# A four-layer network in one kernel: each sequence of the third layer beside the next sequence of the second

## The chip, the cores and the metric

One NeuronCore of a Trainium2 chip (trn2) runs the whole program in one launch. The metric is the device time of the kernel in microseconds (us), the median of the runs. The engines named are TensorE (PE, its weight loads PEld), VectorE (DVE), ScalarE (ACT), GpSimd (POOL) and SyncE (SP, which here only issues DMAs). Each takes its instructions in program order and meets the others at semaphores.

## What is computed

Four layers over `x` of 4 sequences x 512 tokens x 128 features, float32. Each layer normalises its input, computes a mixing branch `s` and a mixture of experts `g`, and adds their product:

```python
for layer in (0, 1, 2, 3):
    xn = layernorm(x)
    x = x + branch(xn) * silu(experts(xn))
```

Layer 0's branch is a selective scan, its experts are dense GELU experts. Layer 1 (the second, "causal"): 16 heads of 8 features, causal softmax attention, projection, residual and a layernorm; four live experts of width 704 with silu gating (22 pieces of 128 hidden units). Layer 2 (the third, "rope"): the numerator of its softmax takes rotated queries and keys, the denominator plain ones,

```python
att_num = exp(q_rope @ k_rope.T * scale)
att_den = exp(q @ k.T * scale).sum(-1, keepdims=True)
```

so all scores are formed twice; then projection, residual, layernorm, and eight experts of width 64. Layer 3: attention with ALiBi bias and capacity-routed top-1 experts over all tokens. A layer works on one sequence at a time and, for layers 0 to 2, needs nothing of the other sequences.

## The kernel before

Everything lies in SBUF: `x`, its normalised form `xn` and the transpose `xnt`. The order of the work is written out by hand: `flow` (L492) makes one list of items `(what, layer, sequence, n)`, and every engine walks that list and does its part of each item. So the list is the program order of all engines at once. The items of layers 1 and 2:

- `a` (layer 1 only): scores of two or four heads into one of two pairs of PSUM banks, whose row maxima DVE takes (`scores_a` L1023, `maxima` L1889). 20 for each sequence. `mx`: the maxima are transposed, split and go through DRAM into the key stacks (SP `maxima` L2220).
- `b`: scores again, to be exponentiated by ACT (`scores_b` L1073, `probabilities` L1470). 20 for a causal sequence. 64 for a rope sequence: for each of 4 head groups (quads) 8 "sums" units (two activations in place that give only row sums, L1480) and 8 rotated units (one activation of 1024 columns into SBUF, L1498).
- `pv`: probabilities times values, four heads side by side in the array, bank PV (`values` L1127); `bc`: transpose and division of a finished quad (L1154, L1919).
- `f`: one expert piece. In layer 1 two 512-column fp32 matmuls into banks MI and UP (L855, L856), a tanh on ACT (L1379), two DVE operations (L1675, L1679), and the down projection of the piece before it (L867). The next `f` may not begin before the second DVE operation has read bank MI. `q`, `v`, `gate` and the mixture's start use MI too.
- `q`: one projected operand, copied by ACT, split by DVE in three bf16 parts (L1867 to L1870), written to DRAM by SP and read back as "stacks" for the score matmuls (`parts_out` L2188, `stacks` L2201). Layer 2 has four, two of them with the rotation.
- `t`: the tail of a sequence in four steps: turn the heads, project (DVE: add, moments), branch norm and combine with the experts, normalise for the next layer and transpose (L1161, L1928, L1942, L1704, L1602, L836).

Layer 1 runs its four sequences one after the other, then layer 2 its four, then layer 3. `schedule` (L348) spreads `f` evenly over the `a` and `b` items, and `TAIL_AT`/`HEAD_AT` (L362) drop the tail of the sequence before and the head of the next between them. The banks are fixed: two pairs alternate over `a` and `b` units (`slot` L721), PV, UP, YB and MI serve the rest. Probabilities lie in two buffers of 4096 columns, `pt` (L587), and a causal quad's last key block in a small third one, `pty`. Layer 2's operands fill four stacks of 2048 columns for all 16 heads.

## Time and profile before

| | us |
|---|---|
| median of 3 runs | 2030.68 (2030.4 to 2031.54) |
| profiled execution | 2028.62 |
| its span | 2026.8 |
| layer 1: last transpose of layer 0 to layer 2's first scores | 493.8 to 1026.4 |
| layer 2: to layer 3's first scores | 1026.4 to 1542.0 |
| PE, DVE, ACT, POOL busy over the span | 1598.5, 1177.7, 1014.9, 209.7 |

The profile is one execution. Busy time of PE is modelled from pipelined matmuls. A view by windows gives the busy time of each engine in a stretch and the granted clock of PE as a share of 2.4 GHz; 0.50 in it is 1.2 GHz. In a timeline an entry is: start, duration, engine, line, operation, output and inputs, shape, count, and in brackets the idle time before it and what ended that. One fp32 matmul is recorded as two instructions.

### The profile page before, as it was taken

The page shows a single profiled execution, that of the slowest core. Times are in us where ns is not written, and L with a number is a line of the kernel's source. Part 1 is how long each engine was busy: PE and PEld are TensorE (multiplying, and loading weights), DVE is VectorE, ACT ScalarE, POOL GpSimd, SP SyncE. Part 2 cuts the span into 40 slices and gives each one's busy share as a digit, 9 for nine tenths or more (in the row PEclk, how much of TensorE's full clock was granted, in tenths as well). Part 3 has the DMA queues.
Part 4 walks back from the last instruction along what each step waited for, and adds up shares of the span by engine and source line. Part 5 has one row for each costly group of instructions (what it writes and reads, how often), then busy time and mean ns, then how long its engine had stood idle before and what let it go on. Part 6 is the DMA issues. An engine that isn't in the chain of part 4 may idle for free.

```text
span 2026.8 us, 24038 instructions
## 1 busy us (share of the span) xinstructions
PE 1598.5 (79%) x8656; PEld 786.6 (39%) x8656; DVE 1177.7 (58%) x2372; ACT 1014.9 (50%) x1658; POOL 209.7 (10%) x152
## 2 busy tenths in 40 slices
PE   5999999886897897888866777677675677786876
PEld 2655555553454444444422223232222322222342
DVE  4789899898646647557534233241225777573522
ACT  4786877772240321313357676666672122332675
POOL 1242423321000000000000000000000000001003
PEclk8999999997999999999978576566666677776999
DMA  5322322453020100100433012021020302021002
GB/s 172 99 79 76 85 73 79 120 136 99 2 63 1 49 17 2 55 8 2 123 110 103 24 32 79 16 82 43 0 67 12 84 28 72 14 72 44 1 2 68
DMA packets 91621, 116.30 MB, mean 57 GB/s; under 512 B 10096, under 2 KB 71536, under 8 KB 91120
## 3 DMA queue, kind: packets, MB, share of 16 engines
q1 hardware_dynamic: 89808, 110.05, 19.1%
q0 software_dynamic: 1696, 4.72, 0.8%
q8 instruction: 70, 1.15, 0.2%
q14 instruction: 47, 0.39, 0.1%
HBM read 83.27 MB, written 31.46 MB: 57 GB/s over the span
## 4 chain that ended last, share of the span: by engine, by line
PE 42%; DVE 19%; ACT 11%; issue 3%; DMA 1%; SPq 1%; POOL 1%; DVEq 0%; POOLq 0%; ACTq 0%
PE ps L1149 9%; PE ps L856 5%; PE ps L867 5%; DVE neg_max L1904 5%; PE ps L855 4%; ACT scratch L1498 4%; ACT ps L1480 3%; PE ps L1062 2%; PE ps L1013 2%; DVE gated L1675 2%; DVE hidden L1679 2%; ACT tanh L1379 1%; DVE mixture_sum L1701 1%; PE ps L1117 1%; ACT weights_even L1498 1%
## 5 line engine op out<-in xcount | busy, mean ns | idle before, releaser
L1498 ACT ACTIVATE scratch<-ps 128x1024 f32<-128x1024 f32 x272 | 274.4, 1021 | 237.3 <-PE ps L1119 61.4
L1904 DVE TENSOR_REDUCE neg_max<-ps 128x2 f32<-128x1024 f32 (+2 forms) x224 | 232.2, 1067 | 102.0 <-PE ps L1062 101.0
L1149 PE MATMUL ps<-scratch,values 128*32 128x512 f32 (+3 forms) x1280 | 186.8, 669 | 11.2 <-ACT scratch L1498 5.7
L1379 ACT ACTIVATE tanh<-ps 128x512 f32<-128x512 f32 x88 | 52.6, 597 | 282.0 <-PE ps L856 282.0
L1480 ACT ACTIVATE ps<-ps 128x512 f32<-128x512 f32 x256 | 150.8, 589 | 60.5 <-PE ps L1108 60.5
L1765 DVE TENSOR_TENSOR_SCAN scratch<-scratch 128x512 f32<-128x512 f32 x128 | 159.5, 1285 | 3.6 <-ACT scratch L1451 3.5
L1675 DVE SCALAR_TENSOR_TENSOR gated<-tanh,ps 128x512 f32<-128x512 f32 x88 | 60.4, 686 | 154.2 <-ACT tanh L1379 154.1
L1917 DVE COPY head_out<-ps 128x512 f32<-128x512 f32 x48 | 33.0, 688 | 191.7 <-PE ps L1149 191.4
L878 PE MATMUL ps<-xnt,weights_even 128*128 128x512 f32 x256 | 127.2, 619 | 7.4 <-ACT gated L1362 6.6
L2085 POOL TENSOR_SCALAR variance_eps<-mean_var 128x4 f32<-128x4 f32 x20 | 5.3, 265 | 1079.0 <-DVE mean_var L1596 1079.0
L855 PE MATMUL ps<-xnt,weights_odd 128*128 128x512 f32 x176 | 105.3, 682 | 12.7 <-DVE hidden L1679 8.7
L867 PEld LDWEIGHTS ps<-weights_odd,hidden 128*128 128x128 f32 x640 | 88.4, 201 | 46.2 <-issue 40.4
L1498 ACT ACTIVATE weights_even<-ps 128x1024 f32<-128x1024 f32 x64 | 65.1, 1024 | 79.9 <-PE ps L1123 79.5
L1117 PE MATMUL ps<-scratch 48*128 48x512 bf16 x256 | 69.5, 516 | 41.9 <-ACT scratch L1498 35.0
L1108 PE MATMUL ps<-scratch 48*128 48x512 bf16 x256 | 73.3, 519 | 37.1 <-ACT ps L1480 36.6
L856 PE MATMUL ps<-xnt,weights_odd 128*128 128x512 f32 x176 | 97.3, 637 | 0.0
L1701 DVE SCALAR_TENSOR_TENSOR mixture_sum<-ps,combine,mixture_sum 128x128 f32<-128x128 f32 x176 | 49.5, 344 | 82.1 <-PE ps L867 82.1
L1062 PE MATMUL ps<-scratch 52*128 52x256 bf16 (+7 forms) x704 | 94.1, 336 | 0.0
L867 PE MATMUL ps<-weights_odd,hidden 128*128 128x128 f32 x640 | 88.6, 284 | 5.0 <-DVE hidden L1679 5.0
L2124 POOL TENSOR_TENSOR weights_odd<-weights_odd,scratch 128x512 f32<-128x512 f32 x32 | 74.7, 2333 | 168.5 <-DVE scratch L1772 168.1
L1048 PE MATMUL ps<-consts,scratch 128*128 128x128 bf16 x256 | 42.5, 257 | 56.9 <-DVE neg_max L1904 56.6
L2124 POOL TENSOR_TENSOR scratch<-scratch 128x512 f32<-128x512 f32 x32 | 67.8, 2120 | 131.8 <-DVE scratch L1772 131.7
(316 smaller groups left out, 2945.2 us busy)
## 6 DMA issues: line engine op xcount, KB each, us to landing
scratch<-state_rows SPq DMA_DIRECT2D x64, 512.0 KB, 4.7
scratch<-parts_scratch SPq DMA_DIRECT2D x288, 96.0 KB, 2.3
parts_scratch<-weights_even SPq DMA_DIRECT2D x168, 128.0 KB, 2.4
weights_odd<-in_l SPq DMA_DIRECT2D x8, 519.5 KB, 6.4
weights_even<-in_l SPq DMA_DIRECT2D x1, 4096.0 KB, 15.7
weights_odd<-in_l SPq DMA_DIRECT2D x1, 4096.0 KB, 14.8
parts_scratch<-gated SPq DMA_DIRECT2D x15, 128.0 KB, 2.4
slots_scratch<-head_out SPq DMA_DIRECT2D x5, 256.0 KB, 5.0
```

The lines of the kernel that those rows point to most:

```text
L855: pe.matmul(ps[:, MI, :], W(l, "w3")[:, P * f:P * (f + 1)], tokens(b), start=True, stop=True)
L856: pe.matmul(ps[:, UP, :], w1, tokens(b), start=True, stop=True).then_inc(q[l, "up_ready"], 1)
L867: mm = pe.matmul(ps[:, YB, P * j:P * (j + 1)], buf[lo:lo + n, P * j:P * (j + 1)], W(l, "w2")[lo:lo + n, P * src:P * (src + 1)], start=(one ...
L878: pe.matmul(ps[:, up_bank(0, n), :], W(0, "w1")[:, P * f:P * (f + 1)], tokens(n // NF[0]), start=True, stop=True).then_inc(q[0, "up_ready" ...
L1062: mm = pe.matmul(place(col + c0, c1 - c0), lhs, stack_of(l, b, 1 + turn)[p0:p0 + KA[l], s, c0:c1], start=False, stop=True, skip_group_chec ...
L1149: mm = pe.matmul(ps[32 * i:32 * i + 32, PV, q0:q0 + n], lhs, buf[:, slot, col:col + n], start=first_, stop=True, skip_group_check=True)
L1480: ins = act.activation(bank, bank, ACT.Exp, accum_out=dens[:, j, h:h + 1])
L1498: act.activation(dst, src, ACT.Exp).then_inc(q[l, "exp_done"], 1)
L1675: own.link(stt(act_g[:, :], act_t[:, :], 1.0, ps[:, UP, :], ALU.add, ALU.mult))
L1765: dve.tensor_tensor_scan(hs[:, g, :], da[n % RING][:, g, :], ub[:, g, :], 0.0, ALU.mult, ALU.add)\
L1904: ins = dve.tensor_reduce(dst, ps[:, base:base + 2, col:col + n], AX.X, ALU.max, negate=True)
L2124: pool.tensor_tensor(y1[b % 2], y1[b % 2], hc[n % 3][:, 1, :], ALU.add)\
```

## The change

`flow` no longer runs layer 1 and then layer 2. After layer 0 it emits `causal_alone` (layer 1, sequence 0), then for b = 1, 2, 3 `causal_beside_rope(b)`, a block with sequence b of layer 1 and sequence c = b - 1 of layer 2, and then `rope_alone` (layer 2, sequence 3). The last quad of a rope sequence and its tail spill into the next block; so does the tail of the causal sequence, on which the rope sequence of the same block depends. `weave` merges lists evenly. What goes with it:

- Score units of both layers alternate over the same two PSUM pairs in list order. Both layers share MI, UP, YB and PV; waits for these banks are now kept in one variable each.
- The two probability buffers become a ring of four buffers of 2048 columns (`ring`, `grain`), filled stage by stage by either layer; a stage is now one key block (one or two for causal).
- Rope sums come before the rotated units in every quad. Layer 2's stacks shrink to two quads (`stack2`); SP loads each quad by an item `ld`, after the quad two before it has been scored. Parts of layer 2 go through two buffers for four operands, in the order q, rotated q, k, rotated k.
- Layer 2's expert pieces become `u2` (up) and `d2` (down and mix, one per expert). Their buffers, layer 2's `heads` and layer 1's combine weights move to free columns of the even weights.
- POOL serves the reciprocal deviations in list order instead of in loops; semaphores are shared by the parity of the layer.

The arithmetic per layer, the matmuls, activations and DVE operations stay the same in number and shape, apart from layer 1's `pv`, which has the same four key blocks in three stages.

```diff
+GRAINS = 4
+OPERAND = {1: (0, 1), 2: (0, 2, 1, 3), 3: (0, 1)}
...
-            for n, hp in enumerate(pairs):
+            for hp in pairs:
                 units_a.append([(h, 3, 512 * k, 512) for k, h in enumerate(hp)])
                 units_a.append([r for k, h in enumerate(hp)
                                 for r in ((h, 2, 512 * k, 384), (h, 0, 512 * k + 384, 128))])
-                units_b.append((len(stages), 2 * n, [(h, 0, 512 * k, 512) for k, h in enumerate(hp)]))
-                units_b.append((len(stages), 2 * n + 1, [r for k, h in enumerate(hp)
-                                                         for r in ((h, 1, 512 * k, 384), (h, 3, 512 * k + 384, 128))]))
-            stages.append((g, "x", len(units_b), 3))
             units_a.append([(h, 1, 256 * n, 256) for n, h in enumerate(by_parity(hs))])
+            for n, hp in enumerate(pairs):
+                units_b.append((len(stages), n, [(h, 0, 512 * k, 512) for k, h in enumerate(hp)]))
+            stages.append((g, [(0, 0, 0, 512)], len(units_b)))
+            for n, hp in enumerate(pairs):
+                units_b.append((len(stages), n, [r for k, h in enumerate(hp)
+                                                 for r in ((h, 1, 512 * k, 384), (h, 3, 512 * k + 384, 128))]))
+            stages.append((g, [(1, 128, 0, 384), (3, 384, 384, 128)], len(units_b)))
             units_b.append((len(stages), 0, [(h, 2, 256 * n, 256) for n, h in enumerate(by_parity(hs))]))
-            stages.append((g, "y", len(units_b), 1))
+            stages.append((g, [(2, 256, 0, 256)], len(units_b)))
+        elif kind == "rope":
+            sums = [[(h, j, 512 * k, 512) for k, h in enumerate(hp)] for j in range(TB) for hp in pairs]
+            units_b += [(None, 0, unit) for unit in sums]
+            for j in range(TB):
+                for n in range(2):
+                    units_b.append((len(stages), n, sums[2 * j + n]))
+                stages.append((g, [(j, 0, 0, 512)], len(units_b)))
...
-def schedule(l):
-    f = [("f", n) for n in range(NF.get(l, 0))]
-    a = [("a", u) for u in range(len(score_units(KIND[l])[0]))]
-    b = b_items(KIND[l])
-    if l == 1:
-        return spread(a, f[:7]) + [("mx", 0)] + f[7:9] + spread(b, f[9:]) + [("fl", 0)]
-    if l == 2:
-        return b[:12] + [("mb", 0)] + b[12:14] + f[:1] + spread(b[14:-16], f[1:]) + [("fl", 0)] + b[-16:]
-    raise ValueError(l)
-TAIL_AT = {1: (1, 4, 32, 47), 2: (1, 3, 6, 10)}
-HEAD_AT = {1: (("q", 0, 36), ("q", 1, 40), ("v", 0, 44), ("gate", 0, 49), ("cw", 0, 52)),
-           2: (("q", 0, 30), ("q", 1, 36), ("q", 2, 42), ("q", 3, 48), ("v", 0, 54), ("gate", 0, 58), ("cw", 0, 62))}
...
+HEAD = {1: (("q", 0), ("q", 1), ("gate", 0), ("cw", 0), ("v", 0)),
+        2: (("q", 0), ("q", 1), ("q", 2), ("q", 3), ("v", 0), ("gate", 0), ("cw", 0))}
...
+def weave(*lists):
+    at_ = [((2 * n + 1) / (2 * len(items)), k, n) for k, items in enumerate(lists) for n in range(len(items))]
+    return [lists[k][n] for _, k, n in sorted(at_)]
+def causal_group(b, g):
+    u = [("b", 1, b, 5 * g + n) for n in range(5)]
+    pv = [("pv", 1, b, 3 * g + n) for n in range(3)]
+    return u[0:4] + pv[0:1] + u[4:5] + pv[1:3], ("bc", 1, b, g)
+def rope_sums(b, g):
+    return [("b", 2, b, 16 * g + n) for n in range(8)]
+def rope_group(b, g):
+    u = [("b", 2, b, 16 * g + 8 + n) for n in range(8)]
+    pv = [("pv", 2, b, 4 * g + n) for n in range(4)]
+    return u[0:4] + pv[0:1] + u[4:6] + pv[1:2] + u[6:8] + pv[2:4], ("bc", 2, b, g)
+def later(items, item, n=2):
+    return items[:n] + [item] + items[n:]
+def causal_alone():
+    a = [("a", 1, 0, n) for n in range(20)]
+    f = [("f", 1, 0, n) for n in range(NF[1])]
+    out = weave(a, f[0:7]) + [("mx", 1, 0, 0)] + f[7:9]
+    main, bc = [], None
+    for g in range(QUADS):
+        group, next_bc = causal_group(0, g)
+        main += later(group, bc) if bc else group
+        bc = next_bc
+    head = head_items(1, 1)
+    return out + weave(main, f[9:], head[:4]) + [("fl", 1, 0, 0), bc] + [("ld", 1, 1, g) for g in range(3)]
+def causal_beside_rope(b):
+    c, p = b - 1, b - 2
+    a = [("a", 1, b, n) for n in range(20)]
+    f = [("f", 1, b, n) for n in range(NF[1])]
+    tail1 = [("t", 1, b - 1, k) for k in range(4)]
+    tail2 = [("t", 2, p, k) for k in range(4)] if p >= 0 else []
+    d = [("d2", 2, p, e) for e in range(4, E2)] if p >= 0 else [None] * 4
+    head1, head2 = head_items(1, b + 1) if b + 1 < NB else [], head_items(2, c)
+    group, bc = rope_group(p, 3) if p >= 0 else ([], None)
+    sums = rope_sums(p, 3) if p >= 0 else []
+    out = [("ld", 1, b, 3), d[0]] + weave(a[0:3], f[0:1], tail1[0:2], sums[0:3])
+    out += [d[1]] + weave(a[3:6], f[1:3], sums[3:8])
+    out += weave(a[6:12], f[3:6], group, tail1[2:4], [("v", 1, b, 0)])
+    out += [f[6], bc, d[2], a[12]] + tail2[0:1] + [head2[0], a[13], d[3]] + tail2[1:2]
+    out += weave(f[7:10], head2[1:5]) + [("ld", 2, c, 0), ("ld", 2, c, 1)] + tail2[2:3]
+    out += weave(a[14:18], f[10:12], head2[5:7], tail2[3:4])
+    group, bc = rope_group(c, 0)
+    out += weave(rope_sums(c, 0), a[18:20] + [("mx", 1, b, 0)], [("mb0", 2, c, 0), ("mb1", 2, c, 0)])
+    d = [("d2", 2, c, e) for e in range(4)]
+    out += [("u2", 2, c, 0), group[0], ("u2", 2, c, 1)] + group[1:3] + [d[0]] + group[3:5] + [d[1]]
+    out += weave(group[5:], f[12:16])
+    group, last = causal_group(b, 0)
+    out += later(weave(group, f[16:17], rope_sums(c, 1)), bc)
+    group, bc = rope_group(c, 1)
+    out += [("ld", 2, c, 2)] + later(weave(group, f[17:18]), last)
+    group, last = causal_group(b, 1)
+    sums = rope_sums(c, 2)
+    out += [d[2]] + later(weave(group, sums[0:4]), bc) + [d[3]]
+    group, bc = causal_group(b, 2)
+    out += later(weave(group, sums[4:8], f[18:20], head1[0:1]), last) + [("ld", 2, c, 3)]
+    group, last = rope_group(c, 2)
+    out += later(weave(group, f[20:22], head1[1:2]), bc)
+    group, bc = causal_group(b, 3)
+    out += later(weave(group, [("u2", 2, c, 2), ("u2", 2, c, 3)]), last) + [("fl", 1, b, 0)] + head1[2:4] + [bc]
+    if b + 1 < NB:
+        out += [("ld", 1, b + 1, g) for g in range(3)]
+    return [item for item in out if item]
+def rope_alone():
+    c, p = NB - 1, NB - 2
+    tail1, tail2 = [[("t", l, b, k) for k in range(4)] for l, b in ((1, c), (2, p))]
+    d = [("d2", 2, p, e) for e in range(4, E2)]
+    head = head_items(2, c)
+    group, bc = rope_group(p, 3)
+    out = weave(rope_sums(p, 3), tail1[0:2], d[0:2]) + weave(group, tail1[2:4])
+    out += [head[0], bc, d[2], head[1], head[2], d[3], head[3]] + tail2[0:1] + [head[4]] + tail2[1:2] + head[5:7]
+    out += [("ld", 2, c, 0), ("ld", 2, c, 1)] + tail2[2:4]
+    next_ = [("set", 3, 0, 0), ("q", 3, 0, 0), ("q", 3, 0, 1), ("v", 3, 0, 0)]
+    d = [("d2", 2, c, e) for e in range(E2)]
+    u = [("u2", 2, c, n) for n in range(4)]
+    beside = [[("mb0", 2, c, 0), ("mb1", 2, c, 0)], u[0:2] + d[0:2], [("ld", 2, c, 2)] + d[2:4],
+              u[2:4] + d[4:6], [("ld", 2, c, 3)] + d[6:8] + next_[0:1], next_[1:2], next_[2:3], next_[3:4]]
+    bc = None
+    for g in range(QUADS):
+        group, next_bc = rope_group(c, g)
+        sums = rope_sums(c, g)
+        out += weave(later(sums, bc) if bc else sums, beside[2 * g]) + weave(group, beside[2 * g + 1])
+        bc = next_bc
+    return out + [bc], [("t", 2, c, k) for k in range(4)]
+def flow():
+    middle, tail = rope_alone()
+    out = first_layer(head_items(1, 0)) + causal_alone()
+    for b in range(1, NB):
+        out += causal_beside_rope(b)
+    return out + middle + last_layer(tail)
...
+        stack2 = [scratch[:, 4096 + 1024 * n:4096 + 1024 * (n + 1)].bitcast(BF16).rearrange("p (s t) -> p s t", t=T)
+                  for n in range(4)]
+        ring = [scratch[:, 8192 + 2048 * n:8192 + 2048 * (n + 1)].rearrange("p (i c) -> p i c", i=4) for n in range(GRAINS)]
...
+        slots, grains, free_when = {}, {}, []
+        for what, l, b, n in steps:
+            if what in ("a", "b") and l in (1, 2):
+                slots[what, l, b, n] = len(slots) % 2
+                stage = units[l][1][n][0] if what == "b" else None
+                if stage is not None and (l, b, stage) not in grains:
+                    grains[l, b, stage] = len(free_when)
+                    free_when.append((l, NS[l] * b + stage + 1))
...
+                def grain_values(l, b, s):
+                    st = units[l][2]
+                    g, regions, end = st[s]
+                    first_ = s == 0 or st[s - 1][0] != g
+                    pe.wait_ge(q[l, "exp_done"], start[l, "exp_done"] + b * NUB[l] + end + 2)
+                    if first_:
+                        pe.wait_ge(*pv_read)
+                        if s == 0:
+                            pe.wait_ge(q[l, "values_ready"], start[l, "values_ready"] + b + 1)
+                    for c, q0, col, n in regions:
                         for i in range(4):
                             h = 4 * g + i
-                            lhs = vx[b % 2][:, c, VW * h:VW * h + 32]
-                            slot = by_parity(range(4)).index(i) if what == "y" else i
-                            mm = pe.matmul(ps[32 * i:32 * i + 32, PV, q0:q0 + n], lhs, buf[:, slot, col:col + n],
+                            place_ = by_parity(range(4)).index(i) if l == 1 and c == 2 else i
+                            mm = pe.matmul(ps[32 * i:32 * i + 32, PV, q0:q0 + n], vx[l - 1][:, c, VW * h:VW * h + 32],
+                                           grain(l, b, s)[:, place_, col:col + n],
                                            start=first_, stop=True, skip_group_check=True)
-                    if part == parts - 1:
-                        mm.then_inc(q[l, "pv_done"], 1)
+                    mm.then_inc(q[l, "pv_done"], 1)
...
+                        place_ = grains[l, b, s]
+                        if n == 0 and place_ >= GRAINS:
+                            from_, count = free_when[place_ - GRAINS]
+                            act.wait_ge(q[from_, "pv_done"], start[from_, "pv_done"] + count + (2 if from_ == 1 else 0))
...
+            def rope_stack(b, g):
+                l, n = 2, QUADS * b + g
+                if n >= 2:
+                    sp.wait_ge(q[l, "b_ready"], 16 * (n - 1))
+                for k in range(4):
+                    sp.wait_ge(q[l, f"parts{k}_out"], 16 * NG * (b + 1))
+                    quad_in(l, b, k, g, stack2[k], 2 * (g % 2), q[l, f"rotated{g}_in" if k >= 2 else f"stack{g}_in"])
...
+            for what, l, b, n in steps:
+                if what == "q" and l < 3:
+                    part_out(l, b, n)
+                    if l == 1 and b == 0 and n == 1:
+                        for g in range(QUADS):
+                            causal_stack(0, g)
+                        sp.wait_ge(xn_ready[0], NB)
+                        load_weights(2)
+                elif what == "ld":
+                    if l == 1:
+                        causal_stack(b, n)
+                    else:
+                        rope_stack(b, n)
+                elif what == "mx" and l == 1:
+                    maxima(1, b)
+                elif what == "t" and l == 1 and n == 3 and b == NB - 1:
+                    sp.wait_ge(xn_ready[1], NB)
+                    load_weights(3)
+                    rows(3)
```

## Rows read from the trace of the kernel before

**Rows 1.** The page: busy tenths of PE, and its clock, in 40 slices.

```profile
PE   5999999886897897888866777677675677786876
...
PEclk8999999997999999999978576566666677776999
```

**Rows 2.** Windows: stretch, length, busy us per engine, PE clock, DMA share, GB/s.

```profile
493.80:1026.40 532.60, 452.20 (x2866) 250.66 (x2865) 321.98 (x657) 144.64 (x192) 7.60 (x12) 0.96 0.12 34
493.80:620.00 126.20, 110.45 (x700) 60.07 (x699) 70.46 (x134) 35.00 (x46) 0.00 (x0) 0.95 0.13 39
1026.40:1542.00 515.60, 364.69 (x1576) 135.20 (x1575) 154.99 (x476) 345.42 (x717) 10.13 (x16) 0.66 0.19 55
626.00:670.00 44.00, 34.55 (x204) 19.42 (x200) 35.30 (x56) 4.35 (x8) 1.27 (x2) 0.92 0.01 1
714.00:758.00 44.00, 39.13 (x278) 22.07 (x274) 17.95 (x35) 14.09 (x18) 0.00 (x0) 1.00 0.07 19
1138.00:1146.00 8.00, 4.98 (x20) 0.74 (x18) 0.00 (x0) 6.52 (x15) 0.00 (x0) 0.50 0.10 32
1170.90:1300.50 129.60, 91.91 (x396) 34.29 (x397) 41.14 (x127) 86.61 (x180) 2.53 (x4) 0.66 0.18 49
```

**Rows 3.** Timeline, PE, layer 1: first and third of three pieces, then scores.

```profile
662.01 1.12 PE L855 MATMUL ps<-xnt,weights_odd 128*128 128x512 f32 x2
...
670.40 1.10 PE L855 MATMUL ps<-xnt,weights_odd 128*128 128x512 f32 x2 [1.33 <-DVE hidden L1679]
...
673.08 0.28 PE L1098 MATMUL ps<-consts 128*128 128x128 bf16 x2
```

**Rows 4.** Timeline, PE, layer 2: sums alone, a dense place, pv at half clock.

```profile
1032.74 0.61 PE L1108 MATMUL ps<-scratch 48*128 48x512 bf16 x2 [0.81 <-ACT ps L1480]
...
1033.95 0.61 PE L1108 MATMUL ps<-scratch 48*128 48x512 bf16 x2 [0.60 <-ACT ps L1480]
...
1063.22 0.39 PE L1108 MATMUL ps<-scratch 48*128 48x512 bf16 x2
...
1114.77 1.93 PE L1149 MATMUL ps<-scratch,values 128*32 128x512 f32 x8
```

**Rows 5.** DVE, layer 1: groups by form; first and last step of a split.

```profile
L1675 DVE SCALAR_TENSOR_TENSOR gated<-tanh,ps 128x512 f32<-128x512 f32 x88 | 60.4, 686 | 154.2 <-ACT tanh L1379 154.1
...
L1904 DVE TENSOR_REDUCE neg_max<-ps 128x2 f32<-128x1024 f32 x32 | 38.9, 1217 | 0.9 <-PE ps L1062 0.9
L1904 DVE TENSOR_REDUCE neg_max<-ps 128x2 f32<-128x768 f32 x32 | 30.4, 950 | 0.1
L1896 DVE TENSOR_REDUCE neg_max<-ps 128x4 f32<-128x1024 f32 x16 | 19.4, 1210 | 0.2 <-PE ps L1062 0.2
L1904 DVE TENSOR_REDUCE neg_max<-ps 128x2 f32<-128x256 f32 x32 | 13.3, 415 | 0.0
...
684.14 0.43 DVE L1867 CAST weights_even<-queries_keys 128x512 bf16<-128x512 f32 x1 [1.97 <-ACT queries_keys L1467]
...
685.79 0.69 DVE L1870 TENSOR_TENSOR weights_even<-queries_keys,weights_even 128x512 bf16<-128x512 f32 x1
```

**Rows 6.** ACT: three exponentials in a row (layer 1); table loads (layer 2).

```profile
673.72 2.85 ACT L1498 ACTIVATE scratch<-ps 128x1024 f32<-128x1024 f32 x3 [0.73 <-PE ps L1114]
...
L1383 ACT ACT_TABLE_LOAD x16 | 20.5, 1283 | 0.3
```

**Rows 7.** Timeline, DVE: first, a middle and last step of layer 1's last tail.

```profile
1031.44 0.69 DVE L1934 TENSOR_TENSOR branch<-ps,weights_odd 128x512 f32<-128x512 f32 x1 [3.31 <-PE ps L1170]
...
1035.97 1.11 DVE L1945 TENSOR_SCALAR branch<-branch,mean_var,rstd 128x128 f32<-128x128 f32 x4 [1.58 <-POOL rstd L2086]
...
1044.99 0.43 DVE L1609 TENSOR_SCALAR branch<-xn 128x512 f32<-128x512 f32 x1
```

**Rows 8.** SP queue: layer 2, four operands out, then back as stacks.

```profile
961.58 31.11 SPq L2199 DMA_DIRECT2D parts_scratch<-weights_even  x24
...
992.80 20.08 SPq L2216 DMA_DIRECT2D scratch<-parts_scratch  x32
```

490 lines of the change are left out of this document (243 added, 247 removed).

## Prediction, made before the change was run

> **What bounds the kernel now.** I read the page's slices first, then windows by layer, then timelines inside them. The slices show three regimes [rows 1]: PE 0.8 to 0.9 busy at full clock up to slice 20, then a stretch of clock digits 5 to 8. Windows put layers on them [rows 2]. Layer 1 takes 532.6 us, with PE 452.2 busy at clock 0.96, DVE 322.0, ACT 144.6. Layer 2 takes 515.6 us, with PE 364.7 busy at clock 0.66, DVE 155.0, ACT 345.4. So layer 1 lives by PE, with ACT nearly free; layer 2 is a mix of ACT and a PE that runs half of its time at 1.2 GHz, with DVE free. The two have different scarce engines, and that is what the change bears on.
>
> PE work is best counted at full clock: busy times clock, 452.2 x 0.96 = 434 us for layer 1 and 364.7 x 0.66 = 241 us for layer 2, so 108.5 and 60.3 us for each sequence. A sequence pair now takes (532.6 + 515.6) / 4 = 262 us for 169 us of such work, a yield of 0.64. Alone, layer 1 yields 434 / 532.6 = 0.81, layer 2 only 0.47.
>
> Inside layer 1 there is a second limit. The first and the third of three expert pieces in a row begin at 662.01 and 670.40 [rows 3]: 4.2 us for one, while PE needs 2.7 us for one (670.40 to 673.08). The rest is the way through tanh and two DVE operations back to bank MI. 22 pieces at 4.2 us are 92 us of a sequence. In the first half of a sequence, where `a` units use DVE, DVE is 35.3 busy of 44 us and PE 34.6 (at 0.92); in the second half PE 39.1 of 44 at 1.00 [rows 2]. In layer 2 sums units come every 1.2 us, set by ACT, with PE 0.61 us at half clock [rows 4].
>
> **What the change removes.** Nothing in work: the same matmuls, activations, reductions, and 8 table loads of 1.28 us for each rope sequence [rows 6] (a GELU and the exponential after it, each piece still by itself). What it can remove is idle time and half-clock time of PE. If three pairs ran together at PE's full-clock work alone they would take 3 x 169 us; nothing lets them go below.
>
> **One block, stretch by stretch.** Prices: causal score unit 0.65 us of PE (an estimate, near the 0.6 that one bias-and-scores unit takes from 673.08 on at full clock), rope unit 0.3 (0.39 with its pipeline [rows 4]), rope `pv` 1.0 (1.93 at half clock [rows 4]), a piece 2.7, `q` or `v` 1.0. On ACT 1.2 for a sums unit, 0.95 for an exponential [rows 6]. On DVE 1.28 for an `a` unit ((38.9 + 30.4 + 19.4 + 13.3) / 80), 1.4 for a piece (twice 0.69), 2.3 for a split (684.14 to 686.48) and 2.1 more (three operations of 0.69) with rotation [rows 5], 14.0 for the tail of a causal sequence (1031.44 to 1045.42 [rows 7]), of which 3.2 wait for POOL (two waits like the 1.58 there).
> (1) Opening to `f` 5: DVE has 12 `a` (15.4), 6 pieces (8.4), the causal tail (10.8 without the waits), values and two expert mixes (some 4): 38.6 us. At the 0.80 busy that DVE reaches in layer 1's first half [rows 2] this is 48; ACT's share (16 rope units, 17 us) hides in it. 47.
> (2) `f` 6 to 9, four `q`, `v`, start of the rope tail: everything but PV work goes through bank MI. Four pieces at 4.2, four `q` and a `v` at about 2, and two rotated splits of 4.4 us that lie on DVE ahead of a piece's operations. In order I get 37 us for 20 us of PE work. 37.
> (3) End of the rope tail, 4 `a`, 2 pieces, gate: DVE 6 + 5.1 + 2.8 + 5 + 1.6 = 20.5. 21.
> (4) Sums of the new sequence: 8 x 1.2 on ACT. 11.
> (5) Two GELUs with four table loads between exponentials (10 on ACT), then four pieces at 4.2. 27.
> (6) The rest, 4 causal quads, 2 rope quads, 16 sums units, 6 pieces: PE 68, ACT 63, DVE 20. At a PE yield of 0.85 (0.89 in layer 1's second half, where only one stream of exponentials had to keep step) 80.
> Sum 223 us at full clock.
>
> **The clock.** Stretches 2 to 4 hold some 35 us of PE work in 69 us. Layer 1's first half held 0.92 with PE 0.79 busy; layer 2 sat at 0.50 in 1138 to 1146 with PE 4.98 of 8 busy, so half that in full-clock work [rows 2]. A stretch at a load of 0.5 lies between the two rows, nearer to the second. Bounds: nothing, or all 35 us doubled (+35). Since ACT and DVE set most of these steps, I add 3 us in full blocks: **226**. The yield is then 169 / 226 = 0.75, between layer 1's 0.81 and today's 0.64. The Trainium skill has the rule behind this (TensorE: Matmul & The Clock Gate, Part 1: The HAM clock gate): the slow clock is the resting state and activity lifts it, so thinning PE's work costs twice. By it alone the block goes as rival D.
>
> **The first block** has no older rope sequence: no spilled quad (8.9 us of PE), no four expert downs, no rope tail on DVE (10.8). 226 less some 20: 206.
>
> **The ends.** `causal_alone` is today's first sequence, 493.8 to 620 [rows 2]: 126. `rope_alone` is worse off than today's last sequence. Today its operands are ready long before. Now a spilled quad (17 us of ACT, an estimated 20 with the causal tail's 14 us and its matmuls beside it), then four `q` with 13.4 us of splits that each wait for their copy (20), then the rope tail, `v` and gate on DVE (17) stand ahead of its first sums, with ACT idle: 57. The 4 MB of layer 3's weights is issued in just that place; bounds nothing to 10 us, and I take nothing, as the splits' DMAs have those 17 us of cover. The main part: today's 129.6 [rows 2] less the head's 5 matmuls of 2 us at half clock, the tail's stall and matmuls (some 14): 104. Sum 161.
>
> **Stacks and SP.** A block issues 36 DMAs of parts, 48 of stacks and 3 of maxima. Issues take 0.4 us when nothing holds them and 0.63 in the run of 32 [rows 8]: at most 55 us in 226, no bound. From the last split to the first sums unit lie 10 issues and two landings, some 10 us, under stretch 3's 21. An item `ld` waits on scores done long before. Behind SP's wait for the maxima stands only the next `ld`, a stretch later. Nothing; if the cover fails, up to 10 a block. The ring of four half-size buffers holds as much as two old ones, and the price of its cross-layer wait is bounded by 0 and by one `pv` (1 us) in 12 stages a block; a gain is excluded as it never frees earlier than its own stage. I take 0. POOL's services in list order are two of 1.6 us as now.
>
> **Sum.** 126 + 206 + 2 x 226 + 161 = 945 against 1048.2 (layers 1 and 2 [rows 2]): 103 less. Layer 3 begins the same way. 2028.6 - 103 = 1925.6 for an execution like the profiled one; the median lies 2.1 above it: 1927.7, so **1928**.
>
> **Rivals.**
> B, the streams decouple better: with four consumers of PE's work the yield rises to 0.85, near layer 1's second half. Full block 199, first 150 / 0.85 = 176, ends 126 + 155: 855, saving 193: 1838. For it: stretches 1 and 6 want different engines. Against: the 4.2 us of a piece and the one bank MI. The Trainium skill goes further (Perfetto Trace Analysis, Identifying the Most-Contended Engine): not matmul busy but weight-load busy shows PE's headroom. By it PE has more than half left in both layers (250.7 of 532.6, 135.2 of 515.6 [rows 2]). That would make a block some 150, bound by DVE and ACT (119 and 122 us for a pair), and the time near 1700; I give this nothing, since three pieces' matmuls in [rows 3] fill their 2.7 us each.
> C, coupling: one order over two pairs means that a DVE unit held up by a tail keeps ACT's next unit out. Yield 0.68: blocks 248, first 222, ends 126 + 170: 1014, saving 34: 1997. This also holds late stacks (three times 10) as its smaller form.
> D, slower: the clock falls through the block. Blocks then keep layer 2's clock 0.66 with PE 0.93 busy, a yield of 0.62: 273, first 250, ends 126 + 175: 1097, costing 49: 2080. It decides from a yield of (3 x 169 - 19) / (1048 - 287) = 0.64. For it: stretches 2 to 4 at half load, and layer 3, also mixed, with clock digits 6 to 9 [rows 1]. Against: layer 1's first half kept 0.92 [rows 2].
> E, the change doesn't do what it says: if every rope item waited on the causal tail of its own block, the layers would run in turn as before, 2030. The tail ends in the first third of a block, so this is thin.
>
> **How the numbers follow.** The chances: forecast 0.60 (blocks of 213 to 240, 1885 to 1970), B 0.14, C 0.14, D 0.09, E 0.03. Range: down to 1855 takes half of B, up to 2000 most of C; left out are some 0.07 below and 0.13 above. 0.2% (4 us) is about what a measurement of this kernel can tell from no change. Faster 0.60 + 0.14 + 0.14 = 0.88, same 0.03, slower 0.09.
>
> **What would show it.** In the changed kernel's windows, from layer 0's last transpose to layer 3's first scores: 945 us; blocks of 206, 226, 226; clock 0.9 over them, lower in each block's second and third stretch; DVE 0.8 busy in each block's first 100 us and under 0.3 after; ACT idle for some 35 us at the start of `rope_alone`. Wrong if the blocks' clock is under 0.75, if PE waits for stack DMAs by more than 10 us a block, or if the blocks' second part is as slow as the first.

## The result, and the profile of the changed kernel

The changed kernel takes **2075.66 us** (median of 4 runs, 2071.7 to 2081.96) against 2030.54 us (2028.87 to 2031.54) for the kernel before on the same chip: a ratio of 1.0232, 95% interval 1.0209 to 1.0256. It is 2.3% slower where the forecast had it 5% faster. The profiled execution spans 2069.9 us, the one before 2026.8: 43.1 us more. Of these 4.5 lie ahead of layer 1's first scores, 35.1 in layers 1 and 2 (1083.3 us against 1048.2 [rows 2]) and 3.5 in layer 3.

The page's slices of TensorE and of its clock, to be laid beside [rows 1]:

```profile
PE   5999899896796678876788776887486677675876
...
PEclk8999999997998878977689786897557568777899
```

Before, layer 1 had a clock digit of 9 throughout, and the low digits stood in layer 2 and in layer 3 behind it. Now digits of 5 to 8 begin with slice 13, where block 1 begins, and run, with a few of 9 among them, through both layers. They have only moved: over both layers the granted clock is 0.81 in either kernel.

Windows of the changed kernel (columns as in [rows 2]): both layers, `causal_alone`, the three blocks, `rope_alone`, then block 2 in the prediction's six stretches:

```profile
498.30:1581.60 1083.30, 829.21 (x4443) 402.76 (x4441) 478.56 (x1137) 492.33 (x908) 18.76 (x28) 0.81 0.14 42
498.30:629.00 130.70, 112.63 (x704) 61.77 (x702) 71.83 (x138) 34.48 (x45) 0.00 (x0) 0.93 0.10 31
629.00:862.00 233.00, 179.29 (x1012) 88.28 (x1011) 107.35 (x249) 105.43 (x189) 2.53 (x4) 0.86 0.15 42
862.00:1135.00 273.00, 211.36 (x1117) 103.70 (x1117) 122.33 (x298) 124.00 (x228) 5.58 (x8) 0.81 0.13 36
1135.00:1408.00 273.00, 209.67 (x1110) 101.99 (x1109) 116.47 (x269) 125.66 (x235) 5.59 (x8) 0.81 0.08 24
1408.00:1581.60 173.60, 116.26 (x505) 47.01 (x506) 60.58 (x188) 102.77 (x212) 5.06 (x8) 0.66 0.29 89
862.00:930.00 68.00, 52.66 (x234) 25.91 (x233) 35.80 (x74) 22.27 (x45) 2.53 (x4) 0.75 0.00 1
930.00:968.00 38.00, 25.12 (x101) 14.54 (x101) 26.21 (x56) 5.89 (x10) 1.79 (x2) 0.82 0.25 67
968.00:997.00 29.00, 17.73 (x87) 10.46 (x86) 19.36 (x64) 3.31 (x8) 1.26 (x2) 0.71 0.27 77
997.00:1012.00 15.00, 10.62 (x40) 4.18 (x38) 4.94 (x7) 10.68 (x30) 0.00 (x0) 0.54 0.01 2
1012.00:1044.00 32.00, 27.45 (x126) 13.81 (x126) 8.67 (x19) 16.40 (x19) 0.00 (x0) 0.79 0.09 26
1044.00:1135.00 91.00, 77.78 (x537) 34.79 (x536) 27.35 (x80) 65.44 (x118) 0.00 (x0) 0.92 0.16 44
```

Block 2 takes 273 us where I had 226. It splits into three terms that will be used throughout: work at full clock 211.36 x 0.81 = 171 us, half-clock time 211.36 - 171 = 40 us, idle 273 - 211.36 = 62 us. A pair of sequences before, from [rows 2], has 204 busy, of which 169 of work and 35 of half-clock time, and 58 idle. So the change removed neither of the two losses. Against the kernel before, most of what it adds over both layers is idle time: 254 us for 231, and busy time 829 for 817.

```profile
493.80:1542.00 1048.20, 816.89 (x4438) 385.86 (x4437) 476.97 (x1133) 490.06 (x909) 17.73 (x28) 0.81 0.15 45
```

Where the half-clock time now falls, by groups of layer 1's up products (first the two of the changed kernel, then the one of the kernel before that answers to L975; columns: group, busy us, mean ns, idle before):

```profile
L975 PE MATMUL ps<-xnt,weights_odd 128*128 128x512 f32 x176 | 125.0, 799 | 17.6 <-DVE hidden L1832 8.5 <-ACT weights_even L1620 6.7 <-DVE values L2043 1.4
L976 PE MATMUL ps<-xnt,weights_odd 128*128 128x512 f32 x176 | 112.4, 726 | 0.0
```

```profile
L855 PE MATMUL ps<-xnt,weights_odd 128*128 128x512 f32 x176 | 105.3, 682 | 12.7 <-DVE hidden L1679 8.7 <-DVE values L1886 1.2 <-ACT queries_keys L1467 0.9
```

The same 88 up products (176 recorded instructions) cost 20 us more. And the timeline of TensorE in block 3 and in `rope_alone` (start, us, instruction, idle before it and what ended it):

```profile
1182.22 1.01 PE L1149 MATMUL ps<-weights_odd,xnt 128*128 128x128 f32 x3 [4.27 <-DVE hidden L1832]
...
1191.75 1.08 PE L963 MATMUL ps<-consts,branch 128*128 128x128 f32 x4 [2.90 <-DVE branch L1762]
...
1223.98 2.08 PE L1143 MATMUL ps<-xnt,weights_even 128*128 128x512 f32 x2 [5.57 <-DVE hidden L1832]
...
1226.80 2.07 PE L975 MATMUL ps<-xnt,weights_odd 128*128 128x512 f32 x2 [0.75 <-ACT weights_even L1620]
...
1251.28 1.03 PE L969 MATMUL ps<-weights_even,xnt 128*128 128x8 f32 x4 [4.05 <-DVE hidden L1832]
...
1471.63 1.08 PE L963 MATMUL ps<-consts,branch 128*128 128x128 f32 x4 [12.96 <-DVE branch L1762]
```

`v` (L1149), `q` (L1143), gate (L969) and the turned normalised input (L963) all need bank MI or the tail's result, and each waits 3 to 13 us for VectorE. Behind such a wait one up product (x2, as it is recorded as two instructions) takes 2.07 us (1.2 GHz); in a dense place it takes 1.12, as in [rows 3]. Added over block 2, waits ended by `hidden` are 18.4 us, by `neg_max` (layer 1's maxima, which free a pair of score banks) 10.1 and by `branch` 6.9; in two sequences of the kernel before (755 to 888 and 1170.9 to 1300.5) they are 5.2, 8.5 and 8.1. What is new is the wait for `hidden`. (The expectations below give 18.9 and 10.8 for the block's `hidden` and `branch`; the trace has 18.4 and 6.9.)

### The profile page after: what moved, and what is told of

It reads as the page before. It is cut to its first block, busy times and chain, and to the rows that moved or that the text cites. A ratio compares the mean times of both kernels' runs of the same rounds, so it can differ in the third digit from the quotient of the medians.

```text
span 2069.9 us, 24003 instructions
## 1 busy us (share of the span) xinstructions
PE 1603.0 (77%) x8656; PEld 804.5 (39%) x8656; DVE 1177.8 (57%) x2370; ACT 1017.4 (49%) x1658; POOL 210.0 (10%) x152
## 4 chain that ended last, share of the span: by engine, by line
PE 38%; DVE 20%; ACT 13%; issue 4%; DMA 1%; SPq 1%; POOL 0%; DVEq 0%; ACTq 0%; POOLq 0%
DVE neg_max L2061 6%; PE ps L975 5%; PE ps L1292 5%; PE ps L995 4%; PE ps L976 4%; ACT scratch L1650 4%; ACT ps L1633 3%; PE ps L1273 2%; PE ps L1192 2%; PE ps L1143 2%; DVE gated L1828 1%; PE ps L1238 1%; PE ps L1242 1%; ACT weights_even L1650 1%; DVE hidden L1832 1%
## 5 line engine op out<-in xcount | busy, mean ns | idle before, releaser
L975 PE MATMUL ps<-xnt,weights_odd 128*128 128x512 f32 x176 | 125.0, 799 | 17.6 <-DVE hidden L1832 8.5
L1292 PE MATMUL ps<-scratch,values 128*32 128x512 f32 (+3 forms) x1024 | 131.1, 604 | 4.3 <-ACT scratch L1650 3.8
L995 PEld LDWEIGHTS ps<-weights_odd,hidden 128*128 128x128 f32 x640 | 98.3, 220 | 52.1 <-issue 51.0
L976 PE MATMUL ps<-xnt,weights_odd 128*128 128x512 f32 x176 | 112.4, 726 | 0.0
L995 PE MATMUL ps<-weights_odd,hidden 128*128 128x128 f32 x640 | 96.2, 300 | 0.7 <-DVE hidden L1832 0.7
L1242 PE MATMUL ps<-scratch 48*128 48x512 bf16 x256 | 61.6, 460 | 38.2 <-ACT scratch L1650 21.7
L1238 PE MATMUL ps<-scratch 48*128 48x512 bf16 x256 | 62.6, 473 | 31.1 <-ACT ps L1633 20.2
L1854 DVE SCALAR_TENSOR_TENSOR mixture_sum<-ps,combine,mixture_sum 128x128 f32<-128x128 f32 x128 | 35.9, 343 | 88.8 <-PE ps L995 88.8
```

Of the source, the lines that this page charges most:

```text
L975: pe.matmul(ps[:, MI, :], W(l, "w3")[:, P * f:P * (f + 1)], tokens(b), start=True, stop=True)
L976: pe.matmul(ps[:, UP, :], W(l, "w1")[:, P * f:P * (f + 1)], tokens(b), start=True, stop=True)\
L995: mm = pe.matmul(ps[:, YB, P * j:P * (j + 1)], buf[lo:lo + n, P * j:P * (j + 1)], W(l, "w2")[lo:lo + n, P * src:P * (src + 1)], start=(one ...
L1238: mm = pe.matmul(place(col, n), stack2[0][p0:p0 + rows_, s % 4, P * c:P * (c + 1)], stack2[1][p0:p0 + rows_, s % 4, :], start=True, stop=True)
L1292: mm = pe.matmul(ps[32 * i:32 * i + 32, PV, q0:q0 + n], vx[l - 1][:, c, VW * h:VW * h + 32], grain(l, b, s)[:, place_, col:col + n], start ...
```

## The experiments

Three theories were open. **Clock**: half-clock time is what the block loses, and would come back if TensorE were kept busy. **Parts**: the ring, the stacks and the quad-wise sums cost, not the order. **Chains**: in one order, VectorE's tail of one layer stands ahead of what the other layer's bank MI needs; TensorE waits, and the clock falls behind the wait.

**The parts without the order.** All of the change, but `flow` gives four sequences of layer 1 (the block's list without layer 2's items) and then four of layer 2 (`rope_in_turn`: four quads as in `rope_alone`, with tail and head of the neighbours beside them).

```diff
+def causal_in_turn(b):
+
+    out = [item for item in causal_beside_rope(b) if item[1] == 1]
...
     out = first_layer(head_items(1, 0)) + causal_alone()
     for b in range(1, NB):
-        out += causal_beside_rope(b)
-    return out + middle + last_layer(tail)
+        out += causal_in_turn(b)
+    for c in range(NB):
+        out += rope_in_turn(c)
+    return out + last_layer([("t", 2, NB - 1, k) for k in range(4)])
```

> The changed kernel with its new parts (ring of four half buffers, stacks of layer 2 apart, quad-wise sums) but the two layers in turn: four sequences of layer 1, then four of layer 2. Clock theory (the changed order costs because thin, gapped TensorE work now also strikes layer 1's fp32 products): layer 1 keeps its granted clock of about 0.95 and some 131 us a sequence, layer 2 some 129 to 140 us at a clock of 0.66, in all 2020 to 2060 us, and layer 1's up products (with the down products behind them) at full clock as before. Parts theory (the ring, the stacks and the sums cost, not the order): 2075 us or more, with the loss inside layer 2's sequences, at 140 us or more each. Order-and-tails theory (VectorE's tails now stand in the path of both layers): like the clock theory here, 2020 to 2060; what tells these two apart are the filled kernels.

Measured 2067.1 us (ratio 1.0184, 1.0158 to 1.0211). One sequence of each layer:

```profile
780.00:933.00 153.00, 118.13 (x719) 65.46 (x718) 80.87 (x170) 35.67 (x48) 2.53 (x4) 0.91 0.08 22
...
1236.80:1355.50 118.70, 85.71 (x396) 31.33 (x396) 40.77 (x127) 86.87 (x180) 2.53 (x4) 0.67 0.19 54
```

All three expectations missed, in the total, which lies 7 us above the one range and 8 below the other, and inside. Layer 2 is 11 us a sequence *faster* than before at the same clock (118.7 against 129.6 [rows 2]), so the parts are a gain there. Layer 1 is 20 us slower, with 35 idle, of which 18.8 for `hidden`: the list that is left when layer 2's items are taken out of a block is a bad one for layer 1. A pair costs 271.7 us here, nearly the block's 273, though nothing is interleaved.

**The same, with layer 1 in its old order.** Heads and tails back at their old places among layer 1's items, `vx` and `faccs` taken by sequence again.

```diff
+    main = weave(a, f[0:7]) + [("mx", 1, b, 0)] + f[7:9] + weave(stream, f[9:]) + [("fl", 1, b, 0)]
...
+        extras += [(-1, ("ld", 1, b, 3))] + [(at_, ("t", 1, b - 1, k)) for k, at_ in enumerate((1, 4, 32, 46))]
...
+        extras += [(at_, item) for at_, item in zip((36, 40, 44, 48, 51), head_items(1, b + 1))]
```

> The layers in turn with the new parts, as in the first of these kernels (layer 2 there took 118.5 us a sequence against 129.6 to 133.4 before), but layer 1's items in the order of the kernel before: heads and tails each at their old places among the scores, two value buffers and two mixture sums taken by sequence. Theory that the interleaving costs and the parts gain: layer 1 takes 131 to 135 us a sequence again instead of 153, layer 2 117 to 121, together 1000 to 1012 us against 1048 before and 1083 with the interleaving, in all 1980 to 2000 us. Parts theory (the ring, stacks and sums cost something in layer 1, and 153 us was theirs): 145 us or more a sequence of layer 1, 2030 us or more in all.

Measured **2009.28 us**, ratio 0.990 (0.9872 to 0.9929): faster than both kernels. The sequences are as expected; the total is 9 us above what was expected, the two layers taking 1017 us. Second sequence of layer 1, second of layer 2:

```profile
624.60:757.00 132.40, 110.18 (x723) 62.12 (x721) 80.61 (x170) 35.61 (x48) 2.53 (x4) 0.97 0.09 25
...
1179.30:1298.90 119.60, 87.44 (x397) 30.96 (x397) 40.87 (x127) 86.99 (x180) 2.53 (x4) 0.67 0.19 53
```

The pair costs 252 us. Beside that, not beside 262, stands the block's 273: the interleaved order costs 21 us a block. The parts theory has fallen. Since the pair of the first kernel in turn costs 271.7 us with the block's order of layer 1 and no item of layer 2 in it, the 21 us need not come from having both layers in one list; they can as well come from where the block puts layer 1's heads, tails and hidden tiles among its scores. These runs do not tell the two apart.

**Which part gains in layer 2.** Its ring cut from four half buffers to two.

```diff
-GRAINS = 4
+GRAINS = 2
```

> The kernel with the layers in turn and tuned (2009 us), but with a ring of two half buffers instead of four. Theory that the ring is what makes layer 2 faster (119.6 us a sequence against 129.6 to 133.4): layer 2 goes back to 128 us or more and the whole to 2045 us or more, layer 1 loses too. Theory that the order of the sums (a whole quad of them ahead of its rotated units) makes it: layer 2 stays within 119 to 123 us, layer 1 loses at most 3 us a sequence, 2009 to 2035 us in all.

2013.07 us (ratio 0.988, 0.9843 to 0.9917), and a sequence of layer 2 takes the same:

```profile
1174.20:1293.70 119.50, 86.89 (x397) 31.02 (x397) 40.86 (x127) 87.00 (x180) 2.53 (x4) 0.67 0.19 53
```

So the ring is not the gain. What is left is the order of the sums (a quad of them ahead of its rotated units, not one by one) with its stacks, and the expert pieces of layer 2, cut into `u2` and `d2` and put at other places: waits for `mixture_sum` are 6.3 us in the old sequence and 0.5 in the new one. None of these was run apart.

**Filling TensorE's queue.** Matmuls by a tile of zeros, added into a bank that TensorE holds anyway, ahead of the long waits; then many more; then the same in layer 2 of the kernel before.

```diff
+            def warm(bank, n):
+                for _ in range(n):
+                    pe.matmul(ps[0:64, bank, :], small[:, 16:48].bitcast(BF16), c16[:, 0:T], start=False, stop=True,
+                              skip_group_check=True)
...
```

> The changed kernel plus matmuls by a weight tile of zeros, 512 columns of bf16 each, added into a PSUM bank that TensorE holds anyway: 6 ahead of each q, 8 ahead of each v, gate and turned xn of layers 1 and 2 (56 to 64 in each of the three blocks, 1 to 2 us ahead of each of those waits). They do no work that is needed. Clock theory: some of the 42 us a block that the half clock costs come back and little is paid, since they run in idle time: blocks at a granted clock of 0.86 to 0.92 instead of 0.81 and 255 to 268 us instead of 273, in all 2020 to 2062 us. Waiting theory (idle time on VectorE's chain is the loss, the clock only follows it): clock up a little, blocks 273 to 285 us, 2075 to 2110 us.

> As the kernel before it, plus one such matmul behind each unit of scores and two behind each down product while a bank is held: about 170 in a block, 37 us of TensorE time at full clock and 73 at half. Clock theory: the granted clock goes to 0.95 or more in the blocks; with 169 + 37 us of work at full clock and 62 us of waits of which half is now filled a block takes 235 to 255 us, in all 1965 to 2025 us. Waiting theory: the added work comes on top, 285 to 310 us a block, 2110 to 2190 us.

> The kernel before with three such matmuls behind each unit of layer 2's scores while the accumulating bank is held, 29 places in a sequence, 87 matmuls, 19 us at full clock and 38 at half. Clock theory: layer 2 gets a granted clock of 0.8 to 0.95 instead of 0.66, but ScalarE (345 us of 516 busy) and its own chain hold its pace: 118 to 129 us a sequence, in all 1985 to 2030 us. Rival (the added time is paid in full, clock or no clock): 135 to 145 us a sequence, 2055 to 2095 us.

Measured 2063.35 us (ratio 1.0164, 1.0145 to 1.0184), 2100.86 (1.0339, 1.0303 to 1.0375) and 2038.94 (1.0049, 1.0028 to 1.0069). Block 2 of the second of them, then its fillers alone:

```profile
885.00:1162.00 277.00, 244.11 (x1291) 114.21 (x1290) 122.69 (x298) 124.29 (x228) 5.59 (x8) 0.88 0.12 35
```

```profile
885.00:1162.00 277.00, 55.73 (x172) 17.29 (x172) 0.88 0.12 35
```

The clock went from 0.81 to 0.88, and the busy time of the needed matmuls from 211 to 244.1 - 55.7 = 188 us: 23 us came back, and 29 of idle time were covered. The fillers' 56 us ate both, since half of them did not land in a wait. The light form is 12 us below the changed kernel by the medians, at the near edge of what the clock theory gave it. In layer 2 of the kernel before the clock rose from 0.66 to 0.78, and the needed busy time fell from 365 to 309 us:

```profile
1026.00:1548.00 522.00, 409.33 (x1914) 155.00 (x1914) 153.91 (x472) 346.52 (x715) 10.13 (x16) 0.78 0.19 55
```

```profile
1026.00:1548.00 522.00, 100.76 (x348) 29.36 (x348) 0.78 0.19 55
```

Yet it takes 522 us instead of 515.6. The clock theory, as a cause that can be treated by itself, missed by 1, by 76 and by 9 us, and the theory of plain waiting missed too, by 9 to 16 us at the other side: a fast clock bought with more work gives little or nothing. The light form, too, brought waits down, those for `branch` in block 2 from 6.9 to 1.5 us.

**The order of the block.** The same 206 items. First: layer 1's scores 4 to 17 stand one by one between the items that use MI, and its `v` and parts of its tail come earlier. Then one step more: the hidden tile and `v` go ahead of layer 2's tail, and layer 2's sums behind it, in the place of layer 1's scores. `t2` and `t3` are parts 2 and 3 of layer 2's tail.

```diff
...
-    out += weave(f[7:10], head2[1:5]) + [("ld", 2, c, 0), ("ld", 2, c, 1)] + tail2[2:3]
-    out += weave(a[14:18], f[10:12], head2[5:7], tail2[3:4])
+    out += [a[10], f[7], a[11], head2[1], a[12], f[8], a[13], head2[2], a[14], head2[3]] + t2
+    out += [a[15], f[9], a[16], head2[4], ("ld", 2, c, 0), ("ld", 2, c, 1), a[17], f[10], head2[5]] + t3 + [f[11], head2[6]]
```

```diff
-    out += [a[10], f[7], a[11], head2[1], a[12], f[8], a[13], head2[2], a[14], head2[3]] + t2
-    out += [a[15], f[9], a[16], head2[4], ("ld", 2, c, 0), ("ld", 2, c, 1), a[17], f[10], head2[5]] + t3 + [f[11], head2[6]]
+    out += [a[10], f[7], a[11], head2[1], a[12], f[8], a[13], head2[2], a[14], head2[3], ("ld", 2, c, 0), ("ld", 2, c, 1)]
+    s = rope_sums(c, 0)
+    out += [f[9], a[15], a[16], head2[4], a[17]] + t2 + s[0:3] + [f[10], s[3], head2[5], s[4], f[11], head2[6]] + t3
     group, bc = rope_group(c, 0)
-    out += weave(rope_sums(c, 0), a[18:20] + [("mx", 1, b, 0)], [("mb0", 2, c, 0), ("mb1", 2, c, 0)])
+    out += [a[18], s[5], ("mb0", 2, c, 0), a[19], s[6], ("mx", 1, b, 0), ("mb1", 2, c, 0), s[7]]
```

> The changed kernel with the same 206 items in a block, in another order in its first 130 us: layer 1's scores 4 to 17 are kept back and put one by one between the items that all use the bank MI (hidden tiles, q, v, gate, turned xn), which in the changed kernel stand right behind each other. Coupling theory (the block loses by chains through one bank: 18.9 us of waits for hidden and 10.8 for branch in block 2, against 5.2 and 8.1 in the two sequences apart): 12 to 18 us of these go, blocks of 254 to 262 us, in all 2020 to 2048 us. Clock theory: the same work spread evenly over the stretch, so a granted clock of 0.85 or more and up to 10 us more back, 2000 to 2030 us. Rival (TensorE's idle time belongs to the sum of the two layers' chains and only moves): 268 to 276 us a block, 2065 to 2085 us.

> The reordered block (259.5 us, 2041 us in all) with one more step: in its trace TensorE waits 11.6 us ahead of v of layer 2, for a hidden tile that VectorE does only after the whole tail of layer 2's sequence before. So that tile and v go ahead of this tail, the stacks are loaded earlier, and layer 2's sums, which only ScalarE has to release, stand behind the tail instead of layer 1's scores, which need VectorE. Coupling theory: 8 to 12 us of this wait go, blocks 2 and 3 at 247 to 253 us and 2015 to 2030 us in all. Rival (the wait moves to the next item that needs VectorE): 257 to 262 us, 2036 to 2046 us.

Measured 2041.4 us (ratio 1.0049, 1.0023 to 1.0074) and 2022.16 us (0.9921, 0.9897 to 0.9945): both times are as the chain theory had them, and the second is below the kernel before. In the first the mechanism was another one. Of the 12 to 18 us that were to go from the waits for `hidden` and `branch`, next to nothing went: they are 18.9 and 5.9 us a block, for 18.4 and 6.9. What fell are the waits for `neg_max`, from 10.1 to 1.3 us: TensorE hardly meets score banks any more whose maxima VectorE has not taken. So the chain through MI was not what this reordering shortened, and its time was right by luck. The second reordering did shorten it: `hidden` fell to 10.4, while `branch` went up to 7.1 and 4.8 us of waiting for layer 2's stacks were new. Block 2 of each:

```profile
855.00:1114.50 259.50, 204.64 (x1119) 99.45 (x1117) 122.15 (x299) 123.85 (x229) 5.07 (x8) 0.82 0.13 37
```

```profile
850.00:1099.90 249.90, 198.71 (x1117) 96.71 (x1116) 121.68 (x297) 123.52 (x229) 5.06 (x8) 0.85 0.14 39
```

How such a chain looks, in the first of the two. TensorE at `v`, and VectorE in the time ahead of it:

```profile
954.03 2.08 PE L1154 MATMUL ps<-weights_even,xnt 128*128 128x128 f32 x8 [11.57 <-DVE hidden L1837]
```

```profile
945.08 1.11 DVE L2107 TENSOR_SCALAR branch<-branch,mean_var,rstd 128x128 f32<-128x128 f32 x4
...
949.13 0.69 DVE L1877 SCALAR_TENSOR_TENSOR x<-branch,x 128x512 f32<-128x512 f32 x1
...
951.47 1.19 DVE L2066 TENSOR_REDUCE neg_max<-ps 128x2 f32<-128x1024 f32 x1
952.58 0.68 DVE L1833 SCALAR_TENSOR_TENSOR gated<-tanh,ps 128x512 f32<-128x512 f32 x1
953.29 0.69 DVE L1837 SCALAR_TENSOR_TENSOR hidden<-gated,ps 128x512 f32<-128x512 f32 x1
```

The two operations that free MI (952.58, 953.29) take 1.4 us, and stand in VectorE's queue behind two splits and the third part of layer 2's tail, which keep it busy without a gap from 937.1 on. In the second kernel the same wait is 3.07 us.

**Fillers again, on the first reordering** (49 in a block).

> The kernel of the reordered block with 47 to 51 matmuls of zero weights added in a block: 3 ahead of each q, v and gate, 4 ahead of each turned xn, one behind each down product while its bank is held. Clock theory: 10 us more of half-clock time go for some 11 us of added matmuls, most of it in idle time: 5 to 10 us a block less than without, 1990 to 2030 us in all. Rival (what is added is paid): the same time as without the fillers or up to 12 us a block more.

2048.75 us (ratio 1.0086, 1.0056 to 1.0115), by the medians 7 us more than without (the two intervals overlap), so the clock theory missed and the rival held. Block 2: clock 0.86 instead of 0.82, and 0.9 us longer.

```profile
862.40:1122.80 260.40, 212.24 (x1168) 101.27 (x1167) 122.17 (x297) 123.83 (x228) 5.06 (x8) 0.86 0.13 37
```

**The same step at the end.** `rope_alone` reordered likewise: sums between gate, tail and turned input, stacks loaded right behind the last `q`.

```diff
-    out += [head[0], bc, d[2], head[1], head[2], d[3], head[3]] + tail2[0:1] + [head[4]] + tail2[1:2] + head[5:7]
-    out += [("ld", 2, c, 0), ("ld", 2, c, 1)] + tail2[2:4]
+    out += [head[0], bc, d[2], head[1], head[2], d[3], head[3], ("ld", 2, c, 0), ("ld", 2, c, 1)] + tail2[0:1] + [head[4]]
+    s = rope_sums(c, 0)
+    out += tail2[1:2] + [s[0], head[5], s[1], head[6]] + tail2[2:3] + s[2:4] + [("mb0", 2, c, 0)] + s[4:6]
+    out += [("mb1", 2, c, 0), s[6]] + tail2[3:4] + [s[7]]
...
```

> The kernel of the second reordering (2022 us; layers 1 and 2 took 1027.8 us, of which 170.9 the last sequence of layer 2 with what is left of the one before it) with the same edit at that last place: there TensorE still waits 3.7, 8.3 and 13.0 us in a row ahead of q, gate and turned xn, for VectorE's tails. Stacks are loaded right behind the last q, v goes ahead of the projection, and the eight sums of the first quad stand between gate, the tail's parts and turned xn. Coupling theory: 15 to 20 us of these 25 go, since the sums need only ScalarE: 151 to 156 us there, 2002 to 2008 us in all. Rival (ScalarE, 101 us busy in 171, or the stacks' transfers take over): 163 us or more, 2013 to 2022 us in all.

2022.14 us (ratio 0.9947, 0.9924 to 0.9971), no gain that can be told from the 2022.16 without it. The rival was right: the waits for `values` went (8.2 us) and those for `branch` fell from 16 to 5 us, and in their place the first sums wait for their stacks:

```profile
1402.32 0.61 PE L1246 MATMUL ps<-scratch 48*128 48x512 bf16 x2 [15.34 <-DMA scratch<-parts_scratch]
```

**How much TensorE's busy time weighs.** One of layer 1's up products shortened, in the changed kernel and in the one before.

```diff
-                pe.matmul(ps[:, MI, :], W(l, "w3")[:, P * f:P * (f + 1)], tokens(b), start=True, stop=True)
+                pe.matmul(ps[:, MI, 0:64], W(l, "w3")[:, P * f:P * (f + 1)], tokens(b)[:, 0:64], start=True, stop=True)
```

> The changed kernel without seven eighths of one of layer 1's two up products: its moving operand is 64 columns instead of 512, the rest of the bank keeps what was there. Those 88 pairs of matmuls take 125.0 us of TensorE's busy time in the changed kernel, so about 109 us go, 27 in each block. Theory that the blocks are bounded by TensorE's busy time (and so by its clock): most of it comes off, blocks of 245 to 255 us instead of 273, 1965 to 2000 us in all. Chain theory (a queue in order, held up by releases from VectorE and ScalarE): the time turns into waits, blocks of 263 us or more, 2035 us or more in all.

> The same cut in the kernel before, where those matmuls take 105.3 us, so about 92 us go, 23 in a sequence of layer 1, where TensorE is busy 112 of 133 us. TensorE bounds that layer by every reading of the trace: 110 to 118 us a sequence, 1945 to 1975 us in all. Should the chain through the bank MI bound it already (a hidden tile every 4.2 us of which TensorE does 2.7), 128 to 133 us a sequence and 2010 us or more.

Measured 2026.67 us (ratio 0.9966, 0.9942 to 0.9991), 49 us below the changed kernel, and 1991.79 us (0.9779, 0.9748 to 0.981), 42 below the kernel before: between both expectations in each. Block 2 of the first, a sequence of layer 1 of the second:

```profile
836.50:1099.20 262.70, 200.55 (x1117) 104.41 (x1116) 122.49 (x297) 123.85 (x228) 5.59 (x8) 0.78 0.13 37
```

```profile
605.70:728.60 122.90, 102.67 (x722) 62.11 (x720) 80.83 (x169) 36.16 (x48) 2.53 (x4) 0.92 0.10 27
```

The shortened product did not shrink to an eighth of its time, as both expectations had assumed: it still takes 343 ns for each recorded instruction, where it took 799. In block 2 its 44 instructions go from 33.75 us to 11.79:

```profile
862.00:1135.00 273.00, 33.75 (x44) 8.28 (x44) 0.81 0.13 36
```

```profile
836.50:1099.20 262.70, 11.79 (x44) 8.37 (x44) 0.78 0.13 37
```

So 22 us of matmuls were cut from the block, and busy time fell by 10.8 (211.4 to 200.6): the other matmuls became 11 us longer. The clock, down from 0.81 to 0.78, is about 7 of these (200.6 x 0.78 of work, at the one and at the other); the rest is open. The time fell by 10.3. In the kernel before 15.8 us a sequence were cut (25.86 to 10.06); busy time fell by 9.6 (from 112.3 in 755 to 888) and the time by 10. Idle time stayed at 62 and near 20. So where needed work is taken out, a block's time follows TensorE's *busy* time, half-clock time included, one for one, on top of an idle time that stays. Added work need not do the same, as 29 of the fillers' 56 us went into waits.

**VectorE's tails.** The first cause was still open: five operations of 0.69 us taken out of the tails of a pair, in both kernels.

```diff
-                    if l == 1:
-                        own.link(tt(sa[:, :, :], sa[:, :, :], xv, ALU.add))
...
-                    own.link(tt(sa[:, :, :], sa[:, :, :], spread_rows(W(l, "gamma")), ALU.mult))
-                    own.link(tt(sa[:, :, :], sa[:, :, :], spread_rows(W(l, "beta")), ALU.add))
+                    if l == 3:
+                        own.link(tt(sa[:, :, :], sa[:, :, :], spread_rows(W(l, "gamma")), ALU.mult))
+                        own.link(tt(sa[:, :, :], sa[:, :, :], spread_rows(W(l, "beta")), ALU.add))
```

> The changed kernel without three of VectorE's operations in each tail of layer 1 and two in each of layer 2 (the multiplication by gamma, the addition of beta and, in layer 1, of the normalised input): 20 operations of 0.69 us, 13.8 us of VectorE in all, 3.5 in each pair of sequences. They stand inside the chains for which TensorE waits ahead of turned xn, v, q and gate. Chain theory with the clock behind it (a wait costs itself and then half-clock time as well): more comes off than is removed, 18 to 30 us, 2046 to 2058 us. Chains at their plain price: 10 to 14 us, 2062 to 2066 us. Rival (VectorE's tails are not what TensorE waits for, busy 122 of 273 us): at most 5 us, 2070 us or more.

> The same cut in the kernel before, the same 20 operations and 13.8 us. There the waits for VectorE's tails are 2.3 us in a sequence of layer 1 and 5.8 in one of layer 2, and layer 1's tail is laid out over 47 places of the order. If the interleaving is what puts the tails on the path, less comes off here than in the changed kernel: 3 to 9 us, 2022 to 2028 us. If both kernels carry them alike, the same 14 to 28 us as there.

The changed kernel falls to 2057.58 us (ratio 1.0139, 1.0103 to 1.0174), 18 us less for 13.8 us of VectorE's work, at the near edge of what the chain theory with the clock behind it gave; the kernel before to 2029.89 us (0.9984, 0.9958 to 1.0009), nothing that can be told. Block 2 of the first:

```profile
855.10:1121.20 266.10, 206.54 (x1118) 101.33 (x1117) 118.94 (x293) 123.99 (x228) 5.59 (x8) 0.82 0.13 36
```

3.4 us less of VectorE and 6.9 us less of block. (This profile is of the fastest of its six runs, the changed kernel's of the fastest of four.) Yet in this block the waits for `hidden` and `branch` did not fall (19.1 and 6.9 us): 2.1 us came off idle and 4.8 off busy time. The waits fell elsewhere. Over both layers, which take 1061.3 us for 1083.3, those for `hidden` are 58.0 us for 67.7, and the first block has the whole of that fall (32.4 to 20.1). What stands is the comparison of the two kernels: the same cut is worth 18 us in one order and, by the interval, between 8.5 and nothing in the other, though VectorE is busy only 122 of 273 us. It shows that this order has VectorE's tails on TensorE's path more than the other had; where on the path, it shows only in part.

## Why the prediction was wrong, point by point

The terms of block 2 in each order (work, half-clock time and idle time, worked out from the windows as above; the clock has two digits, and the work, which is the same in most rows, comes out between 165 and 171 us, so the middle two are good to some 3 us):

| kernel | block, us | work | half clock | idle |
|---|---|---|---|---|
| forecast | 226 | 169 | 3 | 54 |
| changed | 273.0 | 171 | 40 | 62 |
| tails shortened | 266.1 | 169 | 37 | 60 |
| first reordering | 259.5 | 168 | 37 | 55 |
| second reordering | 249.9 | 169 | 30 | 51 |
| changed, many fillers | 277.0 | 215 | 29 | 33 |
| pair in turn, tuned | 252.0 | 166 | 32 | 54 |
| pair in turn, layer 1 in the block's order | 271.7 | 165 | 39 | 68 |
| pair before | 262.6 | 168 | 36 | 58 |

**The failed step is the clock.** "Bounds: nothing, or all 35 us doubled (+35). Since ACT and DVE set most of these steps, I add 3 us." It was 40 us, which is above even the bound: by this account 37 of the 47 us missed. The reason given was the mistake. I took half-clock time to be hidden wherever another engine sets the pace, and looked for it only in stretches 2 to 4. It is 13 us in stretch 1 (52.66 busy at 0.75), 6 in stretch 5 and 6 in stretch 6. In all three TensorE is busy for over three quarters of the time, and stretch 1 has waits of 3 to 4 us in it. And the two shortened kernels show that busy time taken off TensorE comes off the block one for one. The pair before had 36 us of half-clock time already, so the step missed something that was there to be read and that the change left nearly as it was; the forecast had taken it away.

**The second step, idle time**, was 8 us short, and more than that by its cause. Each stretch was priced at the work of its busiest engine: 47 us for stretch 1 from 38.6 us of VectorE. It took 68, with VectorE 35.80 busy, no more than counted. What I left out is the order inside a queue: whose operation stands ahead of the one that frees MI. Stretch 3 (29 for 21) went wrong in the same way. Stretch 2, the only one where I followed items in order, came out at 38 for 37. Stretches 4 and 5 were 15 for 11 and 32 for 27, stretch 6 91 for 80. The first block was 233 for 206, the ends 130.7 for 126 and 173.6 for 161.

**What was right.** Work is unchanged (171 against 169). SP and the stacks cost nothing in the blocks (no wait of TensorE ends at a DMA in block 2). The ring costs nothing (four halves or two) with the layers in turn; in the interleaved order that was not run. `rope_alone` begins with idle time as said, a wait of 12.96 us among it. Of the signs, VectorE was to be 0.8 busy in a block's first 100 us and is 0.57; and neither sign of being wrong that names a number came (clock under 0.75, more than 10 us of waiting for stacks a block), so both stood too far out.

**The rivals.** D was what happened, at 0.09: blocks of 273 (said 273), `rope_alone` 173.6 (175), 2075.7 (2080), though the first block was 233 for 250. Its mechanism was a little off: it had clock 0.66 at 0.93 busy, and measured are 0.81 at 0.77. The yield, 171 / 273 = 0.63, fell below its point of 0.64. So its numbers are partly luck. C had the coupling, but without the clock behind it. They were put as alternatives and go together: in the two reorderings idle time fell by 11 us and half-clock time by 10, and with the tails shortened the two layers lost 10 us of idle and 12 of busy time.

By the Trainium skill's rule (TensorE: Matmul & The Clock Gate, Part 1: The HAM clock gate), the slow clock is the resting state, so thinned work is paid twice. The trace agrees, with 40 us of half-clock time in a block that has 62 us of waits. The Trainium skill's table of advice (same page, Why this matters for your kernels) asks for no idle gaps between bursts of matmuls. The reordered blocks agree, but the heavily filled one shows that closing gaps with added matmuls can return nothing (0.88 and 277 us). By the other rule of the Trainium skill that I weighed (Perfetto Trace Analysis, Identifying the Most-Contended Engine), weight-load busy, beside the share of peak arithmetic, shows TensorE's headroom. Weight loads are busy 403 of 1083 us, which would leave it more than half free. The trace disagrees, since taking matmuls out of the block shortened it by as much as busy time fell (10.3 us for 10.8).

**What stays open.** How much a full clock alone would return was not measured: every filler also lengthened the queue. So the 37 us are an account of where the time stands, not a cause tested by itself. And the tuned order in turn (2009 us) remains 13 us below the best interleaved one (2022 us), though the latter's full block, 249.9 us, is 2 us below the pair's 252: what it loses lies in its first block and its ends. Whether an order exists that gains there too was not found.

## What to carry to other kernels

Before two layers are put into one order, follow each shared bank through the queues: for every item that waits for it, name the operation that frees it and all that stands ahead of that operation on its engine, the other layer's tail above all. A sum of busy times per stretch does not see this. Where TensorE's busy time is on the path, price such a wait at about twice its length. That is an estimate from the two reorderings together (11 us of idle, 10 of half-clock time); each by itself gives another factor (7 and 3 us, then 4 and 7). And compare with the best order of the parts *in turn*: here the parts in turn were worth 1.0% by themselves, and the interleaved order cost 3.3% more.

## What the runs showed of the hardware that I had not expected

- **Cutting work slows the rest.** With 22 us of matmuls cut from a block the granted clock fell from 0.81 to 0.78, and only 10.8 us of busy time went; in layer 1 of the kernel before it fell from 0.96 to 0.92.
- **The clock differs from run to run of one kernel, and the time with it.** In 12 executions of the last reordering the span goes from 2011.4 us (mean clock 0.849) to 2029.9 (0.838), in 17 of the kernel before from 2022.7 (0.839) to 2042.7 (0.827). A straight line through each gives 13 and 14 us for 0.01 of clock. 0.01 of clock is 1575.5 x 0.01 / 0.85 = 18.5 us of TensorE's busy time in the former, so some 70% of half-clock time seems to reach the end. It is a correlation, not a test.
- **A faster clock can be worth nothing.** In layer 2 of the kernel before, 0.66 to 0.78 took 56 us off the needed busy time, and with 101 us of fillers in it the layer took 6 us longer.
